# A Trainium2 transformer kernel: filler waits on the TensorE queue of the tile stage, and three-pass first products of the experts

## The reference, cut to what matters

```python
h = layernorm(x)*(1+ca)+sa;  x = x + ga * attention_16_heads_alibi(h)
h = layernorm(x)*(1+cb)+sb;  x = x + gb * moe(h)        # 8 experts, top 2
h = layernorm(x)*(1+ca)+sa;  x = x + ga * attention_4_heads_with_memory(h)
h = layernorm(x)*(1+cb)+sb;  x = x + gb * local_transformer(h)   # depth 6

# moe: for each expert e:  relu(h @ W1[e] + b1[e]) @ W2[e] + b2[e], times its gate
# local_transformer, six times:
#   qkv = shift(x) @ Wqkv; l2norm, rotary; attention in windows of 32; @ Wo; + x
#   layernorm(shift(x)) @ W1 -> a * gelu(gate) -> @ W2; + x
```

## Time and profile before

| | |
|---|---|
| median of 3 runs | 2114.34 us |
| profiled execution | 2119.18 us, of it span 2117.4 us |
| TensorE matmul busy | 1943.4 us, 92% of the span |
| VectorE busy | 1821.4 us, 86% |
| ScalarE busy | 1546.8 us, 73% |
| GpSimd busy | 1290.5 us, 61% |
| mean granted TensorE clock | 0.984 of full speed |

### The profile page before, as it was taken

How to read it: one execution, slowest core, us unless ns; L and a number is a source line. 1 busy time by engine, 2 the same in 40 slices (tenths; PEclk the granted TensorE clock), 3 DMA queues, 4 the chain that set the end, 5 groups by cost and what they waited for, 6 DMA issues and landing times.

```text
span 2117.4 us, 89360 instructions
## 1 busy us (share of the span) xinstructions
PE 1943.4 (92%) x37572; PEld 1442.3 (68%) x37572; DVE 1821.4 (86%) x3995; ACT 1546.8 (73%) x3028; POOL 1290.5 (61%) x1551
## 2 busy tenths in 40 slices
PE   6888899987788999999999999999999999999996
PEld 4666664455566777777777777777777777777774
DVE  6788775577798999999899999999999998998994
ACT  4777763355576877888788887888878878777873
POOL 1111110000378888788787888878888887777771
PEclk9999999998899999999999999999999999999998
DMA  5000000100232322332333323333233332222321
GB/s 117 2 2 2 2 32 31 61 1 1 58 86 70 79 68 70 93 84 67 78 83 78 87 65 77 86 89 79 67 81 83 87 75 63 73 75 73 77 63 41
DMA packets 99377, 132.62 MB, mean 63 GB/s; under 512 B 29052, under 2 KB 44034, under 8 KB 98978
## 3 DMA queue, kind: packets, MB, share of 16 engines
q1 hardware_dynamic: 98978, 126.90, 23.6%
HBM read 28.20 MB, written 1.11 MB: 14 GB/s over the span
## 4 chain that ended last, share of the span: by engine, by line
PE 48%; DVE 23%; ACT 10%; issue 9%; SPq 5%; POOL 3%; DMA 2%; DVEq 0%; POOLq 0%; ACTq 0%
PE pj L630 15%; PE oo L630 15%; ACT arena L1961 7%; PE sc L630 6%; PE tr L1057 5%; DVE arena L1764 4%; DVE arena L1766 4%; SPq L555 3%; PE tr L633 3%; DMA slab<-arena 2%; DVE bv L1772 2%; DVE arena L1521 2%; DVE small L1795 1%; DVE xn L1353 1%; ACT L1965 1%
## 5 line engine op out<-in xcount | busy, mean ns | idle before, releaser
L1961 ACT ACTIVATE arena<-tr 128x512 f32<-128x512 f32 (+3 forms) x894 | 458.8, 562 | 100.0 <-PE tr L633 51.3
L2397 POOL TENSOR_TENSOR arena<-arena 128x1024 f32<-128x1024 f32 x192 | 457.4, 2382 | 91.3 <-DVE arena L1766 87.5
L1961 ACT ACTIVATE arena<-pj 128x512 f32<-128x512 f32 x576 | 332.5, 599 | 150.9 <-PE pj L630 96.1
L2415 POOL TENSOR_TENSOR arena<-arena,small 128x1024 f32<-128x1024 f32 x192 | 365.6, 1904 | 28.1 <-POOL small L2408 0.9
L1961 ACT ACTIVATE arena<-arena 128x1024 f32<-128x1024 f32 (+4 forms) x446 | 304.6, 693 | 87.6 <-DVE arena L1521 74.0
L1772 DVE TENSOR_REDUCE bv<-arena 128x8 f32<-128x512 f32 x384 | 252.7, 679 | 2.9
L630 PE MATMUL oo<-slab,arena 64*32 64x64 f32 (+1 forms) x12416 | 232.7, 229 | 10.5 <-issue 9.7
L2364 POOL TENSOR_SCALAR rstd<-mv 128x4 f32<-128x4 f32 x40 | 11.4, 284 | 364.5 <-DVE mv L1347 364.4
L633 PE MATMUL tr<-ident,arena 128*128 128x128 f32 x1346 | 206.4, 280 | 19.4 <-DMA beta<-in_L_attn_betas 9.9
L630 PEld LDWEIGHTS oo<-slab,arena 64*32 64x32 f32 (+1 forms) x12416 | 160.8, 106 | 80.0 <-issue 44.4
L633 PEld LDWEIGHTS tr<-ident,arena 128*128 128x128 f32 x1346 | 163.3, 143 | 58.3 <-issue 23.9
(11 more groups left out here) (340 smaller groups left out, 4465.0 us busy)
## 6 DMA issues: line engine op xcount, KB each, us to landing
slab<-arena SPq DMA_DIRECT2D x576, 128.0 KB
slab<-arena SPq DMA_DIRECT2D x336, 64.0 KB
arena<-gate_mem SPq DMA_DIRECT2D x24, 256.0 KB, 4.4
wqkv<-in_L_ffn_Wqkv SPq DMA_DIRECT2D x36, 128.0 KB, 2.5
arena<-in_L_ffn_Wqkv SPq DMA_DIRECT2D x36, 128.0 KB, 2.3
wo<-in_L_ffn_Wo SPq DMA_DIRECT2D x24, 128.0 KB, 2.5
w<-in_L_ffn_W SPq DMA_DIRECT2D x6, 341.0 KB, 3.6
YT<-in_L_attn_x SPq DMA_DIRECT2D x4, 256.0 KB, 3.9
```

Source lines behind the costliest of these rows:

```text
L1961: return nc.scalar.activation(o, i, f, **k)
L2397: p_.tensor_tensor(r_, r_, rb[:, k, :], ALU.add).then_inc(sum_ok, 1)
L2415: p_.tensor_tensor(r3, r3, rs[:, k, :].unsqueeze(2).broadcast_to([P, HL, DL]), ALU.mult).then_inc(qk_rdy, 1)
```

## The change

Two things change. First, TensorE gets filler waits: `spread_out(n)` writes 2n waits on two semaphores (the constants' loads) that have long reached their values, and they become n EVENT_SEMAPHORE instructions, since two waits share one. In slot g >= 8 there are 53, 55, 55 and 34 of them for t = 0 to 3, so that every slot holds 768 instructions (to within 2, and exactly 16 x 768 in a layer); slots 2 to 7 have 70, 66, 66, 67, 67, 48. A third stands after `queries(0)`, a third after `wo_quarter`, the rest after `queries(1)`. In the experts' stage 17 stand in front of each `up(j)` of batch 1.

Second, `up(j)` for batches 1 to 3 uses three passes of float32r in place of one float32 product. ScalarE makes the rounded parts (8 of `mw1`, one for each expert, in batch 0; 3 of the activations), GpSimd the remaining parts (8 and 3), into memory that is free at that time. `up` waits for them with `mw_l` and `h1_l`.

```diff
+SPARE_AT = (53, 55, 55, 34)
+SPARE = {0: 0, 1: 0, 2: 70, 3: 66, 4: 66, 5: 67, 6: 67, 7: 48}
...
+            def spread_out(n):
+
+                for _ in range(n):
+                    pe.wait_ge(ld_const, n_const)
+                    pe.wait_ge(ld_late, n_late)
...
             def up(j):
                 b, n = divmod(j, NE)
+                if b == 1:
+                    spread_out(17)
+                if b >= 1:
+                    pe.wait_ge(mw_l, n + 1)
+                    pe.wait_ge(h1_l, b)
                 for c in range(2):
                     if j >= 1:
                         pe.wait_ge(m_relu, j * 2 - 1 + c)
-                    mm(pj[:, c], mw1[:, n, c * P:(c + 1) * P], H(b)).then_inc(m_h, 1)
+                    w_ = slice(c * P, (c + 1) * P)
+                    if b == 0:
+                        last = mm(pj[:, c], mw1[:, n, w_], H(b))
+                    else:
+                        mm(pj[:, c], mw1_hi[:, n, w_], h1_hi[:, b % 2], stop=False)
+                        mm(pj[:, c], mw1_lo[:, n, w_], h1_hi[:, b % 2], start=False, stop=False)
+                        last = mm(pj[:, c], mw1_hi[:, n, w_], h1_lo[:, b % 2], start=False)
+                    last.then_inc(m_h, 1)
...
+                spare = SPARE.get(g, SPARE_AT[t])
...
                 queries(0)
+                spread_out(spare // 3)
                 if s_.mw is not None:
...
                     wo_quarter(s_.mw, s_.iw)
+                spread_out(spare // 3)
                 if t == 3 and m1 is not None:
...
                 queries(1)
+                spread_out(spare - spare // 3 * 2)
                 if g > 0:
                     crossing(g, 1)
...
+                    if b == 0:
+                        ac.wait_ge(p_tr, B * H0 * T)
+                        act(mw1_hi[:, n], mw1[:, n], ACT.Copy).then_inc(mw_h, 1)
+                    if b < B - 1 and n == 5:
+                        if b >= 1:
+                            ac.wait_ge(m_h, b * NE * 2)
+                        ac.wait_ge(ln_out, NORM_AT["B", b + 1] + 1)
+                        act(h1_hi[:, (b + 1) % 2], H(b + 1), ACT.Copy).then_inc(h1_h, 1)
...
-            for i in range(NORM_AT["B", B - 1], len(NORMS) - 2):
+            def experts_low(n):
+
+                gp.wait_ge(mw_h, n + 1)
+                gp.wait_ge(m_h, n * 2 + 2)
+                p_.tensor_tensor(mw1_lo[:, n], mw1[:, n], mw1_hi[:, n], ALU.subtract).then_inc(mw_l, 1)
+
+            def rows_low(b):
+
+                gp.wait_ge(h1_h, b)
+                p_.tensor_tensor(h1_lo[:, b % 2], H(b), h1_hi[:, b % 2], ALU.subtract).then_inc(h1_l, 1)
+
+            for n in range(4):
+                experts_low(n)
+            power(LNA, NORM_AT["B", B - 1])
+            experts_low(4)
+            experts_low(5)
+            rows_low(1)
+            experts_low(6)
+            experts_low(7)
+            for b in range(2):
+                power(LNA, NORM_AT["C", b])
+                rows_low(b + 2)
+            for i in range(NORM_AT["C", 2], len(NORMS) - 2):
                 power(LNA, i)
```

More of the change, by code:

```diff
@@ L219, in build @@
         mw1 = a.take(NE, FH)
+        mw1_lo = nc.alloc_sbuf_tensor_at("mw1_lo", [P, NE, FH], F32R, offset=arena_at)
         mw2 = a.take(NE, 2, P)
@@ L223, in build @@
         Vh = a.take(T, H0, PADH)
+        mw1_hi = nc.alloc_sbuf_tensor_at("mw1_hi", [P, NE, FH], F32R, offset=arena_at + 4 * a.at)
+        h1_hi = nc.alloc_sbuf_tensor_at("h1_hi", [P, 2, S], F32R, offset=arena_at + 4 * (a.at + NE * FH))
+        h1_lo = nc.alloc_sbuf_tensor_at("h1_lo", [P, 2, S], F32R, offset=arena_at + 4 * (a.at + NE * FH + 2 * S))
         Ssb = a.take(4, S)
@@ L351, in build @@
         gate_out = sem("gate_out")
+        mw_h, mw_l, h1_h, h1_l = sem("mw_h"), sem("mw_l"), sem("h1_h"), sem("h1_l")
         gate_in = [sem(f"gate_in{n}") for n in range(NE)]
```

## The result

The kernel after takes 2238.06 us (median of 4 runs, 2236.24 to 2242.97), the kernel before 2116.61 us (4 runs). The ratio is 1.0575, 95% interval [1.0544, 1.0606]: 121 us slower. The forecast was 2094 us; the time lies above the whole range. The clock is no part of it: 0.985 after, 0.984 before.

A forecast was written before the change was run, and what follows sets the result against it. TensorE alone was taken to bound the experts, TensorE and VectorE in turn the tile stage. 2119.2 - 25 + 11 - 6 = 2099 us profiled, median 4.8 lower: 2094 us; range 2074 to 2107, 8-in-10 range 2070 to 2184.

The forecast's parts named there:

- Part 2, the price of a filler: Tile stage: fillers cost sequencer time only, mostly hidden; at 0.085 us each +11 us, bounds 0 and +104.
- p: Price of one met wait on TensorE's sequencer: taken as 0.085 us, bounds 0.051 and 0.111.
- the prediction's own formula: Third insertion, t = 0 to 2: turn of the probabilities late by 19p + 0.25 - 0.96 us, less 0.75 given back.
- the rival: Tile stage: fillers at p = 0.11 make the probabilities' turn 2 us late where t < 3: 2184 us, chance 0.37.
- Part 2, the two first insertions: Fillers behind the first queries and output projection: hidden at 0.085 us each, 0.6 us late at 0.111.
- Part 2, what comes back: Behind the third insertion, a late TensorE no longer waits 0.36 + 0.23 + 0.18 us for VectorE: 0.75 us a slot.
- Part 1, the fetches: Tile stage: 768-instruction slots fix three borders in about even blocks, nearly all fetch stalls go: -25 us, bounds 0 and -31.
- stalls move with the borders into dense stretches: Tile stage: fetch stalls not saved, 2119 us, or 48 us more at 0.5 us a slot; chance 0.05 with the no-stalls-to-save case.
- the full price: Same as the rival: tile-stage fillers at p = 0.11, 2184 us, chance 0.37.
- Part 3, the experts: Experts' stage, batches 1 to 3: three-pass products shorten each up by 0.28 us, fillers hidden: -6 us, bounds -7 and 0.

The follow-up runs named there:

- e6: Kernel after with only the third filler insertion kept (behind queries(1), none with t = 3), borders moving: 2175.7 us, 1.0270 of before.
- e2: Kernel before with the tile stage's fillers alone, experts unchanged: 2242.6 us, 1.0586 of before.
- e3: Kernel after with 90 instead of 70 fillers in slot 2, so later fetch borders lie 20 instructions earlier: 2234.9 us, 1.0543 of before.
- e5: Kernel after with 22 instead of 34 fillers in slots with t = 3, so the fetch borders move: 2241.2 us, 1.0576 of before.
- e12: Kernel after with fillers placed within the sequencer's lead for each t, 145 in slots 2 to 7, even fixed blocks: 2114.3 us, 0.9986 of before.
- e14: e12 with 22 instead of 34 fillers in slots with t = 3, so the borders move: 2135.2 us, 1.0088 of before.
- e13: e1 run again unchanged, on the same chip as e12: 2113.6 us, 0.9974 of before.
- e1: Kernel after without the tile stage's fillers; the experts' three-pass products and their 136 fillers stay: 2108.5 us, 0.9947 of before.
- e8: e1 without the experts' 136 fillers, so no filler anywhere: 2118.6 us, 1.0003 of before.
- e11: e8 with 34 fillers in each of slots 3, 7, 11 and 15, 136 in all: 2110.8 us, 0.9973 of before.
- e9: Kernel after with fillers spread over six places by the sequencer's slack, 87 in slot 2, more even fixed blocks: 2127.0 us, 1.0053 of before.
- e10: e9's placement with 100 fillers in slot 2 and 22 instead of 34 with t = 3, borders moving: 2146.6 us, 1.0148 of before.

## Why the prediction was wrong

*Part 2, the price of a filler: the step that failed.* The prediction put p at 0.085, between the record's 0.051 and the neighbours' 0.111, "because the runs to be predicted are not recorded ones". It is 0.106 in the trace, and the unrecorded runs are as slow (2236.2 profiled, 2237.1 to 2243.0 not). The row nearest in kind said it, and the argument for going below it had no row behind it. With 0.106 in place of 0.085 the prediction's own formula gives 0.55 us a slot and +40 us for the third insertion alone, where it had 0.15 us and +11. From 0.095 on the rival decided, and it did: 2184 us was its time.

*Part 2, the two first insertions.* They were said to fit, and to cost 0.6 us at 0.111. They cost 0.25 and 0.34 us with t = 0 and 2 but 1.11 with t = 1, where the sequencer has 0.5 us less lead. One slot was read for all four.

*Part 2, what comes back.* 0.75 us was counted; 0.33 to 0.65 came (e6), and in after, between the turn and the slot's end, 0.50, 0.31 and 0.51. The waits of one slot were summed as if a late TensorE got all of them.

Together the fillers' part is +111 us by difference: e2 gives 2242.6 - 2117.2 = 125 us for the whole tile stage, and TensorE has 14 us more of fetch stalls (below). Forecast was +11, with +104 as the upper bound. No run separates the two parts: in e3 35 us of stalls in `values_(1)` went and the time fell by 3 us. The sign that the prediction named for this, slots of 16 us with 1 to 2 us of idle ahead of the turn, is what slot 40 shows.

*Part 1, the fetches: -25 us forecast, 14 us of idle more measured.* The three borders were placed rightly (turn, middle of `values_(1)`, second `window_scores`), but the blocks are 4.1, 4.5 and 7.8 us long, not even: all of a slot's 53 to 55 fillers lie in the third one. And the fetch behind the turn starts late, 2.35 to 2.66 us after the border. By the lines view, issue idle inside dense products was 34 us before (17.5 `sc`, 9.7 `oo`, 5.6 `tr`, 1.4 `pj`) and is 48 after (45.0 `oo`, 2.7 `sc`). With moving borders (e5) the time is the same, so in that kernel the alignment is worth nothing. That a fixed alignment can take the stalls away was right: 21 us between e12 and e14. But no run here makes it pay for its padding. The Trainium skill (Runtime: NRT & Kernel Launch, section on instruction fetch mechanics) has the crossing of a block "mostly hidden"; these two runs and the 44.2 us of issue idle in e14 say that it isn't for dense small products.

The rival "stalls move with the borders into dense stretches", with 48 us and a chance of 0.05, did happen beside the full price, though with e3 and e5 little of it reached the time. It was counted as an alternative to the others, when it could go together with each. The full price's 2184 us had 31 us of fetch gain in it: 2184 + 31 + 14 = 2229, 9 us short of what was measured, and the range ended at 2184.

*Part 3, the experts: right in its stage.* Forecast -6 us; slot 0 starts 5.5 us earlier in after and in e13, 6.5 in e1. TensorE waits nowhere in that stage for GpSimd's or ScalarE's new parts; its waits between 336 and 450 us, all for VectorE, are 1.6 us before and 2.9 in e1. The fillers ahead of `up` cost nothing: the ten steps around batch 1 last 38.0 us with them (e1) and without (e8).

That the medians of e1 and e13 also lie 9 and 4 us under before is in part luck. In their traces the head start is gone at slot 8 (0.4 us ahead in e1, 1.0 behind in e13): the slots 0 to 7 last 133 us against 126.6, with 27 and 24 us at the lower level of the clock against 14. The gain at the end is made in the slots 8 to 94, whose instructions and borders are the same as before: 1345.6 and 1348.9 us against 1357.2, with 19.8 and 20.8 us of issue idle against 27.2. Why the stalls are shorter there stays open.

## What to carry to other kernels

Price a wait, met or not, by the distance of two starts and not by the length of its record, and read the sequencer's lead at each place and in each kind of slot before putting anything on it. A fixed alignment of instruction blocks to a loop body pays only if the padding goes where the sequencer has nothing to do, and, if my reading of the late fetches is right, if each border is passed well before the sequencer's next long wait. In the best case here the padding used up what it gave; always measure it against the same padding with the borders moving. A row of the waits view that names an engine can hide the sequencer: look whether the wait records ahead of the product were met. When two adverse mechanisms can hold at once, the range has to hold their sum.

## What the runs showed of the hardware

- Met EVENT_SEMAPHOREs in a row on TensorE's sequencer start 105 to 106 ns apart, with records of 51 ns (after; 19 of them with 0.7 us of lead made the next product 1.26 us late in e6).
- At borders of blocks of 256 instructions TensorE stood still 46 times in the kernel before, for up to 1.7 us. Around such a stall the fetch began 1.0 to 1.5 us after the border was passed, took 0.9 to 1.6 us, and TensorE went on about 1.4 us after its end. By the sum of the three, 3.3 to 4.5 us (an estimate), a block that goes by faster than that ends in a stall; in e12 one of 3.8 us didn't. Where the sequencer went into a long wait right behind the border (after), the fetch began 2.4 to 2.7 us after it.
- Two placements of the same products over the 256-instruction blocks differ by 8 us here (e8 and e11, 0.4%, intervals just overlapping, with a lower clock in e8), by 19.6 us between e9 and e10 and by 21 between e12 and e14; such an effect can hide or fake a small gain.
